# Vector scalings moved to ScalarE, floors as maxima, and another order of the drain in a gated cross-attention and quantised-FFN block

## The reference

```python
# attention: each query attends to 4 context rows, found by an index
gather = seg_id[:, :, None] - arange(4); neg_mask = gather < 0
k_sel, v_sel = kh[clip(gather, 0, 127)], vh[clip(gather, 0, 127)]
probs = softmax(where(neg_mask, -inf, einsum(q, k_sel) * 0.25))
x = x + tanh(g_xattn) * (einsum(probs, v_sel) @ Wo.T)      # q = layernorm(x) @ Wq.T
# FFN, 256 -> 1024 -> 256
amax = clip(max(abs(w)), 1e-8); w_q = round(w * 127 / amax) * amax / 127       # W_in by column, W_out by row
x_q  = round(x * 32767 / amax(x)) * ...                    # one maximum over the whole tensor
hidden = gelu(quant(layernorm(x)) @ W_in_q + b_in)
x = x + tanh(g_ffn) * (quant(hidden) @ W_out_q + b_out)
```

## Time and profile before

| what | us |
|---|---|
| median of 3 runs (lowest, highest) | 311.67 (310.97, 313.34) |
| the profiled execution, its own time | 311.57 |
| its span, first to last instruction | 309.4 |
| busy in it: PE, DVE, ACT, POOL | 281.3, 276.0, 252.2, 165.7 |

### The profile page before, as it was taken

One profiled execution on the slowest core, in us unless ns is written; L12 is line 12 of the kernel. 1 busy time (PEld: TensorE's weight loads), 2 busy tenths in 40 slices (PEclk: granted clock), 3 DMA queues, 4 the chain that ended last, 5 costly groups with the idle time before them and its releaser, 6 DMA issues.

```text
span 309.4 us, 6195 instructions
## 1 busy us (share of the span) xinstructions
PE 281.3 (91%) x1946; PEld 214.1 (69%) x1946; DVE 276.0 (89%) x523; ACT 252.2 (82%) x514; POOL 165.7 (54%) x144
## 2 busy tenths in 40 slices
PE   6999999999997898998985669999999899999991
PEld 5776787887876787887783534444444688888881
DVE  0899999999999999999989883999998799999991
ACT  2789899899897896788761867999999699999980
POOL 1136899989998799999998203233335001111110
PEclk9999999999999999999999989999999999999997
DMA  7993210000000000000000001013111004444446
GB/s 208 335 407 122 65 51 22 0 2 2 0 3 0 1 2 0 2 0 3 1 1 2 0 0 68 3 78 126 68 68 68 2 0 67 72 68 68 68 68 138
DMA packets 7606, 17.46 MB, mean 56 GB/s; under 512 B 1414, under 2 KB 3918, under 8 KB 7198
## 3 DMA queue, kind: packets, MB, share of 16 engines
q1 hardware_dynamic: 5167, 12.80, 11.3%
q0 software_dynamic: 1008, 3.67, 7.8%
q10 hardware_dynamic: 1407, 0.69, 0.8%
HBM read 7.82 MB, written 7.86 MB: 51 GB/s over the span
## 4 chain that ended last, share of the span: by engine, by line
PE 49%; POOL 21%; DVE 18%; issue 5%; ACT 3%; DMA 2%; ACTq 0%; DVEq 0%; POOLq 0%
PE bank L1043 18%; PE bank L1010 18%; POOL vsel L357 10%; POOL vsel L360 7%; DVE prod L1116 4%; PE bank L830 4%; PE bank L810 3%; DVE bank L1122 3%; POOL o L364 3%; PE bank L788 2%; DMA bin_ld<-in_L_ffn_b_in_dram 2%; POOL rstd L348 1%; POOL both_rstd L345 1%; DVE xres L1172 1%; ACT xn L481 1%
## 5 line engine op out<-in xcount | busy, mean ns | idle before, releaser
L810 PE MATMUL bank<-kvtab,onehot 80*128 80x256 f16 x512 | 64.9, 273 | 5.9 <-ACT vsel L496 3.3
L357 POOL TENSOR_TENSOR vsel<-vsel,pr 128x1024 f32<-128x1024 f32 x31 | 59.9, 1933 | 8.6 <-DVE pr L1152 8.6
L810 PEld LDWEIGHTS bank<-kvtab,onehot 80*128 80x128 bf16 x512 | 48.6, 97 | 18.8 <-ACT vsel L496 5.2
L690 ACT ACTIVATE hidden<-bank,bin__58,zscale 128x512 f32 x64 | 47.8, 789 | 3.8
L1010 PE MATMUL bank<-xhi,win 128*128 128x512 f16 x128 | 49.4, 386 | 1.2 <-ACT win L410 1.2
L1010 PE MATMUL bank<-xlo,win 128*128 128x512 f16 x128 | 49.3, 385 | 0.0
L1478 DVE SCALAR_TENSOR_TENSOR hlo<-hq,rel_wout,hhi 128x512 f16<-128x512 int16 x64 | 45.6, 742 | 0.0
L1422 DVE TENSOR_REDUCE hmax<-hidden (+1 forms) x31 | 36.3, 1213 | 7.4 <-ACT hidden L690 7.0
L360 POOL TENSOR_TENSOR vsel<-vsel 128x512 f32<-128x512 f32 x31 | 39.4, 1273 | 2.4
L389 POOL TENSOR_TENSOR xres<-xres,bout 128x1024 f32<-128x1024 f32 x8 | 18.8, 2358 | 38.8 <-DVE xlo L1417 38.8
L1116 DVE TENSOR_TENSOR prod<-bank,q 128x1024 f32<-128x1024 f32 x32 | 38.8, 1213 | 0.8 <-PE bank L810 0.8
(11 more groups left out here) (165 smaller groups left out, 499.8 us busy)
## 6 DMA issues: line engine op xcount, KB each, us to landing
out_dram<-xres SPq DMA_DIRECT2D x7, 512.0 KB, 2.6
out_dram<-y POOLq DMA_DIRECT2D x7, 512.0 KB, 5.4
xres<-in_x_dram SPq DMA_DIRECT2D x3, 1024.0 KB, 16.5
onehot<-onehot SPq DMA_DIRECT2D x9, 160.0 KB, 2.6
xres<-in_x_dram SPq DMA_DIRECT2D x2, 512.0 KB, 7.0
win_ld<-in_L_ffn_W_in_dram SPq DMA_DIRECT2D x1, 1024.0 KB, 12.8
wout_ld<-in_L_ffn_W_out_dram SPq DMA_DIRECT2D x1, 1024.0 KB, 20.7
wkv_ld<-in_L_xattn_Wkv_dram SPq DMA_DIRECT2D x1, 512.0 KB, 5.2
```

The costliest lines, as they stand in the source:

```text
L357: pool.tensor_tensor(v3, v3, pr[k][:, t].rearrange("p o h -> p (o h)").unsqueeze(2).broadcast_to([P, KW * H, HD]), ALU.mult).then_inc(s_pv, 1)
L690: act.activation(hidden[:, g, f, :], bank, ACT.Gelu, bias=bin_[:, f:f + 1], scale=zscale[:, f:f + 1]).then_inc(s_h, 1)
L810: mm = pe.matmul(dst[:, off * D:(off + 1) * D], onehot[0:U, off, bass.ds(tile * P, P)], kvtab[:, b, part, col:col + D], start=(part == 0), ...
```

## The change

1. `win_levels` and `wout_levels` (DVE): the floor, a `tensor_scalar` maximum with a constant, becomes a `tensor_reduce` maximum over two columns, of which the second holds the constant (`peak_win`, `peak_wout`, filled by two POOL memsets before the loop). The factor 127, the diagonal matrix of W_out's top, the ratio `rel_wout` and the scaling of `bout` become ACT activations. New semaphores tie them.
2. Stage A's orders: on ACT `copy_v(i-1, 0)` goes ahead of `kv_high` and `sums2`, `evac_q` behind `sums2`, and `squares1` of `SECOND1` behind `var_eps`; first-norm piece 10 goes from step 9 to 10, piece 12 joins piece 11 in step 11; `keep_wout8` goes one step later (15 and 16). On DVE `wout_amax` goes behind `shift`, `first_onehot` behind `residual(0)`, `wout_levels` ahead of `stats2`.
3. The drain's orders on PE, ACT and DVE, with four more runs of unread transposes (8, 8, 8 and 6). Pair 15's transposes now stand ahead of pair 12's on PE. The epsilon of pair 15's variance is added on DVE.
4. `weigh_last` writes its products unpermuted, and its reduction reads them permuted (before: the other way round).

```diff
             def round_win(hf):
+                act.wait_ge(s_wilev, hf + 1)
+                v = slice(hf * FC // 2, (hf + 1) * FC // 2)
+                act.activation(sc_win[:, v], sc_win[:, v], ACT.Copy, scale=W_LEVELS).then_inc(s_winsc, 1)
                 act.wait_ge(s_winsc, hf + 1)
...
+            def wout_scales():
+                act.wait_ge(s_wlev, 2)
+                act.wait_ge(s_ident, 2)
+                act.activation(sc_wout[:], sc_wout[:], ACT.Copy, scale=W_LEVELS).then_inc(s_woutsc, 1)
+                act.activation(diag[:], ident[:], ACT.Copy, scale=top_wout[:, 0:1]).then_inc(s_wrow, 1)
...
-            ROUND_AT = {10: 0, 11: 1, 12: 2, 13: 3, 14: 4, 15: 5}
-            FIRST1 = {2: 1, 3: 3, 4: 4, 5: 6, 6: 7, 7: 8, 9: 9, 10: 11, 11: 12}
-            SECOND1 = {2: 2, 4: 5, 9: 10}
+            ROUND_AT = {10: 0, 11: 1, 12: 2, 13: 3, 15: 4, 16: 5}
+            FIRST1 = {2: 1, 3: 3, 4: 4, 5: 6, 6: 7, 7: 8, 9: 9, 10: 10, 11: 11}
+            SECOND1 = {2: 2, 4: 5, 11: 12}
...
             round_win(0)
             evac_oT(NP - 1, 1, ps_q)
+            evac_xn2T(NP - 4, 0)
             norm2(NP - 3, 1)
             var_eps(NP - 2, 0)
-            evac_xn2T(NP - 4, 0)
             half_win(0)
+            round_win(1)
             norm2(NP - 2, 0)
-            var_eps(NP - 1, 1)
             evac_xn2T(NP - 3, 1)
             norm2(NP - 1, 1)
+            keep_win8(0)
+            act.wait_ge(s_tanh, 1)
+            act.activation(bout[:], bout[:], ACT.Copy, scale=tanhs[:, 1:2]).then_inc(s_bias, 1)
+            half_win(1)
             evac_xn2T(NP - 2, 0)
-            round_win(1)
-            half_win(1)
-            keep_win8(0)
             keep_win8(1)
             evac_xn2T(NP - 1, 1)
+            wout_ratio()
...
             transpose_o(NP - 2, 0, (s_p, NP), ps_w)
-            attn_out(NP - 2, 0)
-            transpose_xn2(NP - 4, 0, (s_xn2T, NP - 4))
             pe.wait_ge(s_lastpv, 1)
             win_T(1)
-            pe.wait_ge(s_rel, 1)
+            attn_out(NP - 2, 0)
+            pe.wait_ge(s_oT, NP - 1)
+            idle_work(ps_w, 8)
+            pe.wait_ge(s_wtop, 1)
             transpose_o(NP - 1, 1, (s_q, NP), ps_q)
+            transpose_xn2(NP - 4, 0, (s_xn2T, NP - 4))
+            pe.wait_ge(s_oT, NP - 1)
+            idle_work(ps_w, 8)
             attn_out(NP - 1, 1)
-            transpose_xn2(NP - 3, 1, (s_xn2T, NP - 3))
+            pe.wait_ge(s_oT, NP - 1)
+            idle_work(ps_w, 8)
             pe.wait_ge(s_oT, NP - 1)
             win_back(0)
+            transpose_xn2(NP - 3, 1, (s_xn2T, NP - 3))
+            pe.wait_ge(s_winq, 1)
+            idle_work(bank01[:, 0:512], 6)
             transpose_xn2(NP - 2, 0, (s_xn2T, NP - 2))
...
-                link(dve.tensor_scalar(amax_win[:, v], amax_win[:, v], AMAX_FLOOR, None, ALU.max))
-                link(dve.reciprocal(sc_win[:, v], amax_win[:, v]))
-                dve.tensor_scalar(sc_win[:, v], sc_win[:, v], W_LEVELS, None, ALU.mult).then_inc(s_winsc, 1)
+                link(dve.tensor_reduce(amax_win[:, v], peak_win[:, v, :], AX.X, ALU.max))
+                dve.reciprocal(sc_win[:, v], amax_win[:, v]).then_inc(s_wilev, 1)
...
             def wout_levels():
-                dve.wait_ge(s_ident, 2)
-                link(dve.tensor_scalar(amax_wout[:], amax_wout[:], AMAX_FLOOR, None, ALU.max))
-                link(dve.tensor_reduce(top_wout[:, 0:1], amax_wout[:], AX.X, ALU.max))
-                dve.tensor_scalar(diag[:], ident[:], top_wout[:, 0:1], None, ALU.mult).then_inc(s_wrow, 1)
-                link(dve.reciprocal(sc_wout[:], amax_wout[:]))
-                dve.tensor_scalar(sc_wout[:], sc_wout[:], W_LEVELS, None, ALU.mult).then_inc(s_woutsc, 1)
+                link(dve.tensor_reduce(amax_wout[:], peak_wout[:], AX.X, ALU.max))
+                dve.tensor_reduce(top_wout[:, 0:1], amax_wout[:], AX.X, ALU.max).then_inc(s_wlev, 1)
+                dve.reciprocal(sc_wout[:], amax_wout[:]).then_inc(s_wlev, 1)
...
-            residual(NP - 3, 1)
             softmax_end(NP - 1, 1)
-            stats2(NP - 3, 1)
             weigh_last(NP - 1, 1)
+            residual(NP - 3, 1)
+            stats2(NP - 3, 1)
+            aggregate(NP - 3, 1)
+            norm_bias(NP - 4, 0)
             win_amax(0)
             win_levels(0)
-            norm_bias(NP - 4, 0)
-            aggregate(NP - 3, 1)
-            wout_ratio()
+            wout_top()
             residual(NP - 2, 0)
-            largest(NP - 4, 0)
             stats2(NP - 2, 0)
             norm_bias(NP - 3, 1)
+            largest(NP - 4, 0)
             aggregate(NP - 2, 0)
             win_amax(1)
             win_levels(1)
...
             norm_bias(NP - 2, 0)
             stats2(NP - 1, 1)
             aggregate(NP - 1, 1)
+            dve.wait_ge(s_mv, dve_pairs(NP - 1) + 1)
+            dve.tensor_scalar(ve[1][:], mv[1][:, :, 1], LN_EPS, None, ALU.add).then_inc(s_ve, 1)
             largest(NP - 3, 1)
+            norm_bias(NP - 1, 1)
             largest(NP - 2, 0)
-            norm_bias(NP - 1, 1)
             norm2_half()
-            dve.tensor_scalar(bout[:], bout[:], tanhs[:, 1:2], None, ALU.mult).then_inc(s_bias, 1)
             dve.wait_ge(s_xn2b, 1)
             largest(NP - 1, 1)
```

64 lines of the change are left out of this document (37 added, 27 removed).

## The result

| | before | after |
|---|---|---|
| median (lowest, highest), us | 312.50 (310.97, 313.60), 4 runs | 304.51 (304.18, 304.74), 4 runs |
| profiled execution; span | 311.57; 309.4 | 304.32; 302.5 |
| busy: PE, DVE, ACT, POOL | 281.3, 276.0, 252.2, 165.7 | 282.8, 271.6, 253.2, 166.0 |

The ratio is 0.9747, 95% interval 0.9697 to 0.9797: faster.

What follows compares the result with a forecast made beforehand. The prediction took POOL to bound stage A's second half, held up by DVE's late levels, and a chain through all engines to bound the drain. 311.57 - 2.7 (stage A) - 2.4 (drain), clock 0, gave 306.5 us, range 304.7 to 309.3.

Steps and rivals of the forecast that it cites:

- Part 1: Stage A, step 9: W_out's shorter levels on DVE remove POOL's wait, saving 2.7 us, bounds 1.0 to 2.83.
- None to POOL: Stage A: ACT's fuller steps 10 and 11 delay DVE about 0.5 us and POOL not at all; counted 0, up to 2.5.
- at 0, bounds 0.3 either way: Stage A: moving `copy_v`, `evac_q`, `first_onehot` and `wout_amax` costs nothing, hidden by a nearly always busy PE in early steps.
- Part 2: Drain: earlier levels and new orders bring pair 15's projection and the first quantised x earlier, saving 2.4 us, bounds 1.0 to 2.9.
- a sign of being wrong: Drain: DVE's last reduction, in steps of 1024 bytes, taking 2 us; 1.2 was taken, bounds 1.2 and 2.07.
- Late next: ACT: Drain: ACT's list, some 6.6 us, makes it next to be late for pair 15, with a cover of only 0.1 us.
- Part 3: Clock from 183 to 187 us: it stays fallen as before, counted 0; a full clock would give 0.9 us.
- The full clock: Rival: the clock stays at 2.4 GHz, 0.9 us faster, 305.6 us; chance 0.16.
- Stage A's loss: Rival: ACT's fuller steps 10 and 11 replace DVE's stall, up to 2.5 of the 2.7 goes, 309.0 us; chance 0.10.
- Held as before: Rival: the new reductions on DVE are still held by POOL, one hold of up to 1.76 stays, 308.2 us; chance 0.07.
- the drain's loss: Rival: ACT's list or the unread transposes hold pair 15, so the drain gains nothing, 308.9 us; chance 0.11.
- ScalarE as the bound: Rival: ACT's added 4.5 us is uncovered and the drain gives nothing, so slower, 313.4 us; chance 0.06.

Runs made afterwards that it cites:

- e3_wout_back: The kernel after with W_out's levels (floor, diagonal, factor 127) again as scalings on DVE; median 309.50 us, ratio to before 0.9926.
- e6_probe: The kernel after with one small unread DVE instruction added three times a step in steps 9 to 15, another kind each step; 320.13 us in one execution.
- e1_kinds_only: The kernel before with only the new kinds of instruction for both levels, `rel_wout` and `bout`, orders and `weigh_last` as before; median 306.50 us, ratio 0.9821.
- e5_act_steps_back: The kernel after with ScalarE's (ACT's) order in stage A and its three tables as before; median 304.09 us, ratio to before 0.9750.
- e10_stage_a_back: The kernel after with both ScalarE's order and tables and VectorE's (DVE's) order in stage A as before; median 303.97 us, ratio to before 0.9782.
- e2: The kernel after without its four new runs of unread transposes; median 305.63 us, ratio to before 0.9783.
- e7: The kernel after without the first two of its four new runs of unread transposes; median 305.78 us, ratio to before 0.9789.
- e9_both: The kernel after with ACT's stage A as before, and an unread run, DVE's pair 15 epsilon and W_in's second rounding moved; median 306.33 us, ratio 0.9806.
- after_again: The kernel after run once more, no edit; median 305.62 us over 6 runs, ratio to before 0.9791.
- e8: The kernel before with only the four new runs of unread transposes added to its old drain; median 311.44 us, ratio to before 0.9994.
- e0_before: The kernel before run once more, no edit; median 311.58 us over 10 runs, ratio 0.9979, profiled execution 310.07.
- e4: The kernel after with W_in's levels again as scalings on DVE, with the factor 127 there; 305.51 us in one run.

## Why the prediction was right in its steps and wrong in its number

**What bounds.** Right: POOL in the second half of stage A, the chain through all engines in the drain, and DVE's scalings held to the end of POOL's instruction (e3_wout_back, e6_probe).

**Two terms failed.** The sum held nothing for the execution's ends (behind the last `y`, and outside the span), and they gave 1.51 us: this is the larger, and it is what took the result out of the range. The sum held 0 for the clock, with a reason that doesn't carry, and it gave 0.86. In stage A a third was mis-sized without much effect on the number: the moves of orders, put at 0, took 0.5 to 0.6.

**Part 1, 2.7 forecast, 2.38 measured.** The new instructions took 0.38 us instead of 0.6, and the reductions weren't held. The kinds alone gave 2.98 (e1_kinds_only), above the upper bound of 2.83. Of that, 2.7 is the wait the sum was about, just as forecast, and 0.3 is POOL's later start at 63 us, which nothing in my list explains. "None to POOL" for ACT's fuller steps 10 and 11 was right, for POOL waits for nobody behind 99.77. The step that failed is the one before it, that the moves of `copy_v`, `evac_q`, `first_onehot` and `wout_amax` are hidden "at 0, bounds 0.3 either way": ACT's order took 0.2 to 0.3 and DVE's another 0.3, in steps 4 and 5 (e5_act_steps_back, e10_stage_a_back). That the whole came within 0.3 of the forecast is luck in part: the unexplained 0.3 covers half of what the orders took.

**Part 2, 2.4 forecast, 2.5 measured.** Less the 2.38 by which all of it starts earlier, the projection of pair 15 came 2.3 earlier (forecast 2.2), the residual 2.4 (2.2), the last maximum 2.5 (2.4). Pair 15's transposes started 0.10 after POOL's tile (166.69 to 166.79), at POOL's limit. The row names `top_wout` as what ended the wait, but that had ended at 166.31 (166.15 + 0.16). The reduction with steps of 1024 bytes took 1.94, not the 1.2 that I took: the wrong end of my bounds. It was named as a sign of being wrong, and cost nothing, as the forecast also said: POOL's tile came later than what hung on it. The unread transposes cost 0.1 (e2, e7), not up to 0.5. I had seen that the weight would no longer be the last to come, and had not made a term of it; its 0.37 is given back at the second piece of x. "Late next: ACT" didn't come true in the kernel after: there pair 15's bias waited 0.23 for POOL's `rstd`, and its last maximum for nobody. ACT was the next to be late once DVE's list was changed: 0.35 in e9_both, and 0.37 in e1_kinds_only.

**Part 3, 0 forecast, 0.86 measured.** The price of the fall was right (0.9, and 0.85 between two profiles of the kernel before); the choice of 0 was wrong. The forecast took the fallen clock of one execution as the kernel's own and let it stay. In fact it differs from execution to execution of the kernel before (granted 0.969 to 0.997 in 62), and all 20 of the new drain with its unread transposes were granted 0.994 to 1.000 (after, after_again, e5 and e10). How much of that is the transposes' is open: e8 shows them to end the low clocks in the old drain, but the profile of e2 has the new drain without them and no fall. In the profiled pair this is 0.86. On medians it is more: the 62 executions of before have a median of 311.8, the 12 of them with the highest clock 310.0. My reason for 0 (3.06 us of PE work went before no fall, 3.36 before one) compared two stretches of one execution. e0_before has the same list and 3.39 us of work in the stretch of the second, and no fall, so such a pair of rows could not decide it. By the Trainium skill, TensorE: Matmul & The Clock Gate, Part 1, activity releases the throttle; the clocks of e8 against before agree in direction, though I had set the rule aside.

**The sum.** 311.57 - 2.38 - 2.49 = 306.70 is what the schedule alone gives, 0.2 from the forecast. The clock takes it to 305.84. That is inside the range. What took it out are the last 1.51 us: 1.16 behind the last `y` and 0.35 outside the span. The 1.16 is mostly a draw: the kernel before showed a tail of 5.77 in e0_before and 6.55 here, and the kernel after 5.39 and 5.68. The 0.35 is not: time less span was 2.11 to 2.29 in all 68 executions of the kernel before and 1.78 to 1.84 in all ten of the kernel after, so it goes with the kernel. It is 2.13 to 2.22 again where either half of the levels is back on DVE (e3, e4), and 2.03 to 2.12 in e9_both; why stays open. I had made no term and no width for either, and the range's lower end, 304.7, left 0.9 below the sum for a full clock. Against the repeated kernel after (305.62) the forecast is 0.9 off; ten executions of after have a median of 304.7, at the edge of the range. So that the first four fell outside it is in part their draw.

**The rivals.** The full clock came true in the profiled execution, and was given 0.16. Stage A's loss was real but 0.5 to 0.6 us of the 2.5, and not by the fuller steps that the rival named. "Held as before" is refuted by W_in's levels at 165.56 and by e6_probe; the drain's loss and ScalarE as the bound are refuted by D and by the total.

## What to carry to other kernels

Where a short VectorE instruction shows a length that changes from place to place, compare its end with GpSimd's; if they agree to some hundredths, use a form that isn't held (one column, a reduction, a reciprocal) or another engine. Take the start, the tail and the clock of one execution as a draw and not as a property, until more executions show which it is: cut the profile at instructions that both kernels have, and put what varies into the range. Test a reordering without the edit that it came with: here the kinds gave 4.24 us and stage A's new orders took 0.5 to 0.6 of it back, because an instruction that had filled a wait was moved behind it.
